# Attention sums in 64-key parts, one per row half of the matmul array, sharing one accumulator bank

## The reference

```python
xn = _layernorm(x, axis=-1)                       # x: (2, 4096, 256)
# attention: 16 heads of 16 dimensions
qkv = (xn @ W_qkv + b_qkv).reshape(B, D, 3, H, p).transpose(2, 0, 3, 1, 4)
scores = softmax(einsum('bhip,bhjp->bhij', q, k), axis=-1)      # no scaling
out = einsum('bhij,bhjp->bhip', scores, v).reshape(B, D, N)
# feed-forward part
h = butterfly(einsum('bsd,dh->bsh', xn, W_exp) + b_exp, up_weights)   # 256 -> 1024, 10 stages
h = butterfly(gelu(h + up_bias), down_weights)
y = einsum('bsh,hd->bsd', h, W_con) + b_con + down_bias
result = x + out + y
```

## Time and profile before

| | |
|---|---|
| median of three runs | 5605.22 us (5603.41 to 5609.47) |
| span of the profiled execution | 5607.5 us |
| PE busy (matmuls) | 5554.5 us, 99% |
| PE weight loads | 2628.7 us, 47% |
| ACT busy | 5021.6 us, 90% |
| DVE busy | 4884.1 us, 87% |
| POOL busy | 527.8 us, 9% |
| granted TensorE clock, mean | 0.995 |

### The profile page before, as it was taken

The page is one execution under the profiler, slowest core; times in us unless marked ns, Lnnn a source line. Parts: engine busy times, 40 slices in busy tenths (PEclk is TensorE's granted clock), DMA queues, the critical chain, the costliest instruction groups (busy, mean ns, idle before and its releaser), DMA issues.

```text
span 5607.5 us, 98374 instructions
## 1 busy us (share of the span) xinstructions
PE 5554.5 (99%) x36132; PEld 2628.7 (47%) x36132; DVE 4884.1 (87%) x9092; ACT 5021.6 (90%) x9744; POOL 527.8 (9%) x482
## 2 busy tenths in 40 slices
PE   7899999999999999999999999999999999999999
PEld 6644444444444444444444444444444444444698
DVE  7799999999999999999999999999999999998233
ACT  6699999999999999999999999999999999999644
POOL 2436652000000000000000000000000000000000
PEclk9899999999999999999999999999999999999999
DMA  8702221111110111111111011111111101110111
GB/s 297 218 25 48 58 58 29 17 19 21 21 21 8 21 21 21 21 15 21 21 21 20 8 21 21 21 21 15 21 21 21 17 10 21 21 21 2 35 45 41
DMA packets 212351, 197.12 MB, mean 35 GB/s; under 512 B 149288, under 2 KB 170152, under 8 KB 200104
## 3 DMA queue, kind: packets, MB, share of 16 engines
q1 hardware_dynamic: 208432, 168.05, 15.9%
q0 software_dynamic: 3456, 23.07, 1.1%
HBM read 128.07 MB, written 60.82 MB: 34 GB/s over the span
## 4 chain that ended last, share of the span: by engine, by line
PE 96%; DVE 0%; issue 0%; DMA 0%; ACT 0%; SPq 0%; DVEq 0%; ACTq 0%
PE psum L1055 36%; PE psum L1019 32%; PE psum L1041 20%; PE psum L1142 3%; PE psum L1157 3%; PE psum L998 0%; DVE probs L856 0%; DMA q_rows<-neg_rows 0%; ACT probs L774 0%; PE psum L1073 0%; PE psum L1028 0%; PE psum L1080 0%; DVE maxima L856 0%; ACT L774 0%; DVE y L965 0%
## 5 line engine op out<-in xcount | busy, mean ns | idle before, releaser
L774 ACT ACTIVATE probs<-psum 128x512 f32<-128x512 f32 x8192 | 4222.8, 606 | 297.3 <-PE psum L1041 296.7
L847 DVE TENSOR_REDUCE maxima<-psum 128x1 f32<-128x512 f32 x6042 | 3958.3, 686 | 373.9 <-PE psum L1019 258.1
L1019 PE MATMUL psum<-k_rows,q_rows 48*128 48x512 f32 x7049 | 2497.4, 453 | 0.7 <-ACT spill L790 0.6
L1055 PE MATMUL psum<-probs,v_cols 128*32 128x512 f32 x16384 | 2184.2, 605 | 0.0
L1041 PE MATMUL psum<-q_rows,k_rows 50*128 50x512 f32 x8192 | 2058.5, 423 | 3.5 <-DMA q_rows<-neg_rows 3.5
L1019 PEld LDWEIGHTS psum<-k_rows,q_rows 48*128 48x128 f32 x7049 | 1175.4, 184 | 1244.0 <-DVE maxima L843 815.3
L1041 PEld LDWEIGHTS psum<-q_rows,k_rows 50*128 50x128 f32 x8192 | 1268.8, 185 | 126.0 <-ACT probs L774 33.2
L843 DVE CUSTOM_DVE_ANT_0 merged<-psum,spill 128x512 bf16<-128x512 f32 x1007 | 686.9, 682 | 1.8 <-issue 1.0
L790 ACT ACTIVATE spill<-psum 128x512 f32<-128x512 f32 x1007 | 602.0, 598 | 16.0 <-PE psum L1019 13.9
L1055 PEld LDWEIGHTS psum<-probs,v_cols 128*32 128x32 f32 x16384 | 322.5, 108 | 617.9 <-issue 323.7
L1019 PEld LDWEIGHTS psum<-k_diff,q_rows 48*128 48x128 f32 x1007 | 184.5, 183 | 845.7 <-DVE maxima L847 790.8
(11 more groups left out here) (106 smaller groups left out, 2154.0 us busy)
## 6 DMA issues: line engine op xcount, KB each, us to landing
q_rows<-q_parts SPq DMA_DIRECT2D x384, 128.0 KB, 4.4
k_rows<-k_parts SPq DMA_DIRECT2D x192, 128.0 KB, 7.1
q_parts<-parts SPq DMA_DIRECT2D x32, 512.0 KB, 6.4
k_parts<-parts SPq DMA_DIRECT2D x32, 512.0 KB, 4.1
planes<-in_up_planes POOLq DMA_DIRECT2D x10, 1024.0 KB, 6.7
planes<-in_down_planes POOLq DMA_DIRECT2D x10, 1024.0 KB, 5.0
y<-in_x SPq DMA_DIRECT2D x16, 512.0 KB, 5.1
xn_transposed<-xnt SPq DMA_DIRECT2D x16, 512.0 KB, 5.9
```

The costliest lines, as they stand in the source:

```text
L774: nc.scalar.activation(probs[:, 2 * (u % 2) + half, BANK * g:BANK * g + BANK], ps_s[:, r % 4, :], ACT.Exp).then_inc(s_exp, 1)
L847: nc.vector.tensor_reduce(largest, region(use), axis=AX_X, op=ALU.max).then_inc(s_region_free, 1)
L1019: nc.tensor.matmul(region(use_of[n, j]), q_rows[m % 4][lower:lower + ROWS, P * t:P * t + P], keys[lower:lower + ROWS, :], start=True, stop ...
L1055: last = nc.tensor.matmul(ps_o[VW * g:VW * g + VW, :], v_cols[:, KT * (head % 2) + UNITS * half + at, :], probs[:, 2 * (u % 2) + half, BAN ...
```

## The change

The sums of a key block are split in two parts of 64 keys. Part n uses rows 64n to 64n + 63 of the array, of `v_cols` and of `probs`; both add to the same bank 7. A part waits until the part before it, which is in the other rows, is complete (`s_pv` becomes two semaphores). The order of a unit becomes four equal quarters: a part of the sums in one half of the rows, then two pieces and two scores in the other half. The halves in `PIECE` and `SCORE` are arranged for that, and key half 1 now comes before key half 0. Besides, the folding of the weights on GpSimd takes 7 instructions a row instead of 6 and one buffer less.

```diff
-    WEIGHT_OPS = 36
+    FOLD_OPS = 7
+    WEIGHT_OPS = 6 * FOLD_OPS
...
-        PIECE = [(1, 0), (1, 1), (0, 0), (1, 2), (0, 1), (0, 2), (1, 3), (0, 3)]
-        DIFFERENCE, MERGED = 3, 6
+        PIECE = [(1, 0), (1, 1), (0, 0), (0, 1), (1, 2), (1, 3), (0, 2), (0, 3)]
+        DIFFERENCE, MERGED = 4, 5
...
-        SCORE = [(r // 2 % 2, 2 * (r // 4) + r % 2) for r in range(2 * QG)]
+        SCORE = [(1 - r // 2 % 2, 2 * (r // 4) + r % 2) for r in range(2 * QG)]
...
-        s_pv = sem("probs_used")
+        s_pv = [sem(f"probs_used_in_rows_of_half{n}") for n in range(2)]
...
-                        chain(nc.gpsimd.tensor_tensor(a, tmp(0), tmp(1), add))
...
+                    if step == 2:
+                        chain(nc.gpsimd.tensor_tensor(tmp(1), tmp(0), tmp(1), add))
...
+                    if step == 6:
+                        chain(nc.gpsimd.tensor_copy(a, tmp(1)))
...
                     if g == 0 and u >= 2:
-                        act.wait_ge(s_pv, 2 * (u - 2) + half + 1)
+                        for n in range(2):
+                            act.wait_ge(s_pv[n], 2 * (u - 2) + 2 - half)
...
                 def turn(s):
-                    dve.wait_ge(s_pv, KT * s + KT)
                     if s > 0:
                         dve.wait_ge(s_evac, s)
+                    dve.wait_ge(s_pv[1], KT * s + KT)
...
-                def sums(u, half):
+                def sums(u, half, n):
                     s, at = divmod(u, UNITS)
                     head = s // 2
-                    if at == 0 and half == 0:
+                    rows = slice(HALF_P * n, HALF_P * n + HALF_P)
+                    if at == 0 and half == 1 and n == 0:
                         if s > 0:
                             pe.wait_ge(s_o_free, s)
                         pe.wait_ge(s_vc[head % 2], 16 * IN_ROW * (head // 2 + 1))
                     pe.wait_ge(s_exp, 2 * QG * u + LAST_OF_HALF[half] + 1)
+                    if n == 1 or half == 0 or u > 0:
+                        pe.wait_ge(s_pv[1 - n], 2 * u + n + (1 - half))
                     for g in range(QG):
-                        last = nc.tensor.matmul(ps_o[VW * g:VW * g + VW, :], v_cols[:, KT * (head % 2) + UNITS * half + at, :],
-                                                probs[:, 2 * (u % 2) + half, BANK * g:BANK * g + BANK],
-                                                start=(at == 0 and half == 0), stop=(at == UNITS - 1 and half == 1))
-                    last.then_inc(s_pv, 1)
+                        last = nc.tensor.matmul(ps_o[VW * g:VW * g + VW, :], v_cols[rows, KT * (head % 2) + UNITS * half + at, :],
+                                                probs[rows, 2 * (u % 2) + half, BANK * g:BANK * g + BANK],
+                                                start=(at == 0 and half == 1 and n == 0), stop=(at == UNITS - 1 and half == 0 and n == 1))
+                    last.then_inc(s_pv[n], 1)
...
-                    piece(n, 0)
-                    score(u + 1, 0)
-                    piece(n, 1)
-                    score(u + 1, 1)
-                    score(u + 1, 2)
-                    piece(n, 2)
-                    score(u + 1, 3)
-                    sums(u, 0)
-                    piece(n, 3)
-                    piece(n, 4)
-                    score(u + 1, 4)
-                    score(u + 1, 5)
-                    piece(n, 5)
-                    score(u + 1, 6)
-                    score(u + 1, 7)
-                    piece(n, 6)
-                    piece(n, 7)
-                    sums(u, 1)
+                    for quarter in range(4):
+                        sums(u, 1 - quarter // 2, quarter % 2)
+                        piece(n, 2 * quarter)
+                        score(u + 1, 2 * quarter)
+                        piece(n, 2 * quarter + 1)
+                        score(u + 1, 2 * quarter + 1)
```

More of the change, by code:

```diff
@@ L485, in attention_and_butterfly_ffn @@
         planes = sb("planes", [P, 2, 4, PAIRS], until=before_ffn)
-        fold = sb("fold", [P, 3, PAIRS], until=before_ffn)
+        fold = sb("fold", [P, 2, PAIRS], until=before_ffn)
         merged = sb("merged", [P, BANK], BF16, until=before_ffn)
@@ L518, in use @@
             by_scalar.append(int(not vector))
-            bank_of.append(n % 7 if n < 2 * PAIRS_OF_TILE * PAIRED else 4 + n % 3)
+            bank_of.append(n % 7 if n < 2 * PAIRS_OF_TILE * PAIRED else SCORE_BANKS + n % REGION_BANKS)
             use_before.append(last_in.get(bank_of[n]))
@@ L605, in turned_weights @@
         def turned_weights(m):
-            return psum[:, 4 + m % 3, 0:D]
+            return psum[:, SCORE_BANKS + m % REGION_BANKS, 0:D]
         def wait_for_stores(engine):
@@ L642, in fold_weights @@
                 def fold_weights(k):
-                    n, r = rows_of_turns[k // 6]
+                    n, r = rows_of_turns[k // FOLD_OPS]
                     w, _, _, s = turns[n]
@@ L655, in tmp @@
                         return fold[:, q, :].rearrange("p (n s) -> p n s", s=stride)
-                    if k % 6 == 0:
+                    step = k % FOLD_OPS
+                    if step == 0:
                         if r == 0:
@@ L665, in fold_weights @@
                         chain.done += 1
-                    if k % 6 == 1:
-                        nc.gpsimd.tensor_tensor(tmp(1), b, plane(0, 1), mult).then_inc(s_fold, 1)
-                        chain.done += 1
-                    if k % 6 == 2:
-                        chain(nc.gpsimd.tensor_tensor(tmp(2), a, plane(1, 0), mult))
-                    if k % 6 == 3:
-                        chain(nc.gpsimd.tensor_tensor(a, tmp(0), tmp(1), add))
[L673 to L676, removed]
+                    if step == 1:
+                        chain(nc.gpsimd.tensor_tensor(tmp(1), b, plane(0, 1), mult))
+                    if step == 2:
+                        chain(nc.gpsimd.tensor_tensor(tmp(1), tmp(0), tmp(1), add))
+                    if step == 3:
+                        nc.gpsimd.tensor_tensor(tmp(0), a, plane(1, 0), mult).then_inc(s_fold, 1)
+                        chain.done += 1
+                    if step == 4:
+                        chain(nc.gpsimd.tensor_tensor(b, b, plane(1, 1), mult))
+                    if step == 5:
+                        nc.gpsimd.tensor_tensor(b, tmp(0), b, add).then_inc(s_fold, 1)
+                        chain.done += 1
+                    if step == 6:
+                        chain(nc.gpsimd.tensor_copy(a, tmp(1)))
                 def scale_and_add(s):
@@ L687, in _ @@
                 for s in range(SUPER):
-                    for k in range(WEIGHT_OPS * s, min(WEIGHT_OPS * s + WEIGHT_OPS, 6 * len(rows_of_turns))):
+                    for k in range(WEIGHT_OPS * s, min(WEIGHT_OPS * s + WEIGHT_OPS, FOLD_OPS * len(rows_of_turns))):
                         fold_weights(k)
@@ L727, in _ @@
                         if s > 0:
-                            sp.wait_ge(s_pv, KT * s)
+                            for n in range(2):
+                                sp.wait_ge(s_pv[n], KT * s)
                         load_v(head, head % 2)
@@ L771, in exp @@
                     if g == 0 and u >= 2:
-                        act.wait_ge(s_pv, 2 * (u - 2) + half + 1)
+                        for n in range(2):
+                            act.wait_ge(s_pv[n], 2 * (u - 2) + 2 - half)
                     act.wait_ge(s_score, 2 * QG * u + r + 1)
                     nc.scalar.activation(probs[:, 2 * (u % 2) + half, BANK * g:BANK * g + BANK],
-                                         ps_s[:, r % 4, :], ACT.Exp).then_inc(s_exp, 1)
+                                         ps_s[:, (2 * QG * u + r) % SCORE_BANKS, :], ACT.Exp).then_inc(s_exp, 1)
                 def rectify_pair(n, i):
@@ L815, in _ @@
                 act.wait_ge(s_bias, 1)
-                act.wait_ge(s_pv, 2 * UNITS_ALL)
+                for n in range(2):
+                    act.wait_ge(s_pv[n], 2 * UNITS_ALL)
                 def step(c, i, p, first):
@@ L1037, in score @@
                         pe.wait_ge(s_neg_in, 2 * 16 * (s + 1))
-                    if e >= 4:
-                        pe.wait_ge(s_exp, e - 3)
+                    if e >= SCORE_BANKS:
+                        pe.wait_ge(s_exp, e - SCORE_BANKS + 1)
                     lower, key = HALF_P * half, P * (u % UNITS)
-                    nc.tensor.matmul(ps_s[:, r % 4, :], k_rows[s // 2 % 2][lower:lower + ROWS + MAX_PARTS, key:key + P],
+                    nc.tensor.matmul(ps_s[:, e % SCORE_BANKS, :], k_rows[s // 2 % 2][lower:lower + ROWS + MAX_PARTS, key:key + P],
                                      q_rows[s % 4][lower:lower + ROWS + MAX_PARTS, BANK * g:BANK * g + BANK],
                                      start=True, stop=True).then_inc(s_score, 1)
-                def sums(u, half):
+                def sums(u, half, n):
                     s, at = divmod(u, UNITS)
                     head = s // 2
-                    if at == 0 and half == 0:
```

(2 more changed lines are left out.)

6 lines of the change are left out of this document (3 added, 3 removed).

## The result

The changed kernel takes 16444.3 us (median of four runs, 16443.7 to 16447.8) against 5605.4 us (5603.4 to 5609.5): 2.93 times the time, with an interval of 2.929 to 2.938. The forecast of 5400 us and its range of 5230 to 5730 us are far off, and on the wrong side. The profiled execution has a span of 16446.0 us.

A forecast was written before the change was run, and what follows sets the result against it. Bound: full-width sums blocks alternating with bursts of pieces and scores, ScalarE and VectorE near their limits. 4.56 + 0.11 = 4.67 us a unit against 4.875, over 1005 units, gave 5400 us; range 5230 to 5730.

The forecast's parts named there:

- They fit beside a part: Attention on TensorE: two pieces and two scores of the other row half, 1.15 us, run while a sums part runs.
- Rival 1: Sums parts beside pieces and scores: different tile shapes don't run together; quarter 2.14 us, 9350 us in all; chance 0.15.
- A 64-row pass takes a 128-row pass's time: Sums on TensorE: halving the rows doesn't shorten a pass; two passes take 1.07 us, bounds 0.54 to 1.07.
- The hand-over: Between successive sums parts on TensorE: each waits until the one before is complete, 0.07 us, at most 0.15.
- Rival 2: Completion of a part to the next part's load takes longer: decides at 0.12 us; at 0.15, 5728 us; chance 0.14.
- The start of a super: First part waits for the transpose, 1.3 us, plus 0.5 us of VectorE's small operations: 1.8 us in 16 units.
- What it would cost uncovered: Seventh weight-folding instruction on GpSimd: expected without a price; 65 us if other waiting didn't cover it.
- Rival 3: TensorE matmuls start strictly in order, pieces only behind a part's second pass: quarter 1.60 us, 7140 us; chance 0.02.
- 1.14 us a quarter: Attention, a quarter of a unit: 1.07 us for the part plus 0.07 us waiting for its predecessor; unit 4.56 us.
- three and four banks of work: Work ahead of VectorE and ScalarE, 1.2 to 1.9 us, covers one quarter, so the chain of parts sets the unit.

The follow-up runs named there:

- pairing alone: The changed kernel with its 64*32 parts, but each piece beside a score of the other row half: 13078 us, mean clock 0.522.
- twins alone: The changed kernel plus, beside each part, a same-shaped part in the other rows into bank 6, two piece banks instead of three: 16555 us, mean clock 0.518.
- late-parts kernel of the old order: The kernel before with each sums call as two 64-row parts back to back, but whole sums in its first 128 units: 12131 us.
- twins-and-pairs kernel: The changed kernel with pieces beside scores of the other half, a same-shaped extra part in the other rows beside each part, two piece banks: 7795 us.
- kernel with late parts: The changed kernel, but with whole sums in its first 320 units and 64-row parts only from there on: 13499 us.

## Why the prediction was wrong

**The step that failed: "They fit beside a part."** The forecast put two pieces and two scores beside a 64*32 part of the other half. They don't run beside it at all. At the upper clock a quarter is 0.99 + 1.15 = 2.14 us, as Rival 1 had it, and as was measured where a part ran at that clock. The shape decides, not the rows: with 64*128 parts the same program starts the piece 0.02 us after the part. The trace of before had a sign of it, and the prediction gave both readings: the score of the upper half, whose rows and bank were free, stood still until the other shape was through, either for the shape or because it stood behind a score that had to wait. Whole sums in the new order show a matmul passing one of the other half that comes before it, which speaks against the second reading. The first was weighed at 0.15 and should have weighed most. The Trainium skill (TensorEngine Tiling (Array Packing), Key Properties) says that a change of tiling mode drains TensorE; the runs agree, with 0.99 us of a part before the other shape may start, against 0.02 us within one shape.

**The second failure: the clock stood in no case.** The sum, all rivals and the range took the 1.00 of before as given. Rival 1's mechanism was the right one, and its 9350 us is 7094 us short of the measured 16444. Nearly all of that difference is the lower clock: quarters of 3.86 instead of 2.14 us, times 4096, are 7045 us. So of the 10839 us lost, some 3745 are worked out for the exclusion at the upper clock (9350 - 5605), and some 7090 for the clock. The first of these two is an estimate from one measured quarter, the kernel never having run whole at that clock.

**What falls out of what.** Exclusion and clock appear as one chain. Because nothing runs beside a part, and the change had taken apart the pairs of pieces and scores in the belief that a part would be their partner, half of the rows stands idle at every moment. In the table, pairing alone leaves the clock down, twins alone (with a bank less) leave it down, and both together bring it up. That idle rows are the reason is a reading of these four, which others contradict in part (below).

**Steps that held.** A 64-row pass takes a 128-row pass's time: the part holds the array for 0.99 us as four whole sums did. The hand-over: in the late-parts kernel of the old order, at the upper clock, the second part's weight loads start 1.15 us after the first's, 1.07 of work and 0.08 of wait; 0.07 was forecast, and Rival 2 needed 0.12. Eight such waits stand between 887 and 914 us, 8.0 us in all.

```profile
886.97 0.15 PEld L1063 LDWEIGHTS psum<-probs,v_cols 64*32 64x32 f32 x8 [0.36 <-DVE o_t L890]
...
888.12 0.15 PEld L1063 LDWEIGHTS psum<-probs,v_cols 64*32 64x32 f32 x8 [0.99 <-PE psum L1063]
```

In the kernel after it isn't on the path at all: the part before is through by the time that four other matmuls have run, and only three weight loads of L1066 in the whole run wait for a sums matmul, 0.5 us in all. The start of a super: 1.8 us were forecast, and 1.7 us is the wait of TensorE for the transpose in the twins-and-pairs kernel, 109.8 us in 64 supers. The two are near each other by luck as much as by the account, since that kernel's quarter is another one; in the kernel after the wait is 60.7 us, under 1 us a super.

```profile
L1073 PE MATMUL psum<-probs,v_cols 64*32 64x512 f32 x32768 | 4417.5, 609 | 111.6 <-DVE o_t L899 109.8
```

POOL's busy time rose by 24 us (527.8 to 551.6), and no line of POOL is on the chain. (What it would cost uncovered was put at 65 us; 6 times 1.29 us in nine supers are 70.) Rival 3, strict order, is refuted by whole sums in the new order. There the Trainium skill (TensorE: Matmul & The Clock Gate, Part 3) has matmuls strict in start, and this trace again disagrees: a piece at 4003.86, the score before it in the program at 4004.05.

**Terms that didn't get to count.** "1.14 us a quarter" is 1.31 at the upper clock where the shapes allow it (a fourth of the 5.24 us of the wide parts, whose width differs from the change's), which is no gain over 4.875. The step that fails there is that "three and four banks of work" cover a quarter, so that the chain from part to part sets the unit: parts wait for exponentials and exponentials for scores. The margin per quarter was 0.08 us (1.22 - 1.14), less than this one step missed.

**What stays open.** What exactly holds the clock down. Idle rows go with it in the four kernels of the table. But the kernel before with one bank less, 10542 us, has whole sums and many pairs and is at 0.50 too, while whole sums in the new order, 6999 us, are at 1.00 with more matmuls of one half alone. Nor does the pace divide them: the kernel with one bank less fell from the upper clock while its unit took some 6.1 us, and whole sums in the new order stay up at 6.18, with the same matmuls in a unit. That the missing bank slows the pieces is seen (6.1 against 4.875 us at the upper clock); that the clock falls for it is only argued. All these kernels had one run.

## What to carry to other kernels

Before splitting a matmul to run it beside another, look whether the two have the same tile shape, columns as well as rows. 64*32 parts and 64-row tiles of 128 columns took turns here, and each turn cost the whole block. Keep matmuls of the two row halves in pairs, even where the sum of their times says that it doesn't matter, and price every reordering also at the lower clock: here that was twice the loss of the mechanism itself. A second look at one short row of the profile, an operation that was free to start and didn't, would have been worth more than the rest of the sum.

## What had not been expected of the hardware

- TensorE can have work recorded for 99% of the time and be granted 1.2 GHz for 15.8 ms on end. The Trainium skill (TensorE: Matmul & The Clock Gate, Part 1) says that activity releases the throttle and calls the low state the idle one; by busy time this trace disagrees, 99% at 0.50.
- More work can be faster: 32768 narrow passes added to the kernel of 13078 us gave one of 7795 us, with one PSUM bank less for the pieces.
- One PSUM bank less for the pieces took the kernel before from 5609 to 10542 us, all of the attention at the lower clock but for a stretch of 44 us.
- With twice the clock a quarter of the changed kernel is 1.8 times as fast, not twice: 2.14 us (one quarter, in the kernel with late parts) against 3.86.
